# Gated experts, attention and routed experts on one core: x1's return moved ahead of expert 6's stores, output positions held in registers, and a new VectorE order in attention with v's bias folded

## The chip, the cores and the metric

One core of one Trainium2 chip runs one launch. The metric is the device time in microseconds (us). Engines: PE is TensorE, ACT is ScalarE, DVE is VectorE, POOL is GpSimd, SP is SyncE (it only issues DMAs). A "q" behind an engine's name is its instruction queue (register work, DMA issues).

## The reference

```python
x = x + attention(gated_ffn(x, type))                 # 64 sequences of 64 tokens, width 256, 16 heads, causal
x = x + moe(shared_and_typed_ffn(x, type))            # 3 shared and 2 typed passes, 4 gates
# attention:
q, k, v = x @ Wq.T + bq, x @ Wk.T + bk, x @ Wv.T + bv
o = softmax(q k / 4, causal) @ v
return o @ Wo.T + bo
# moe: a three-layer router, top 2 of 8 experts, at most 10 tokens of a sequence per expert
out = sum(scale * (relu(x @ eW1 + eb1) @ eW2 + eb2))  # over the two chosen experts
```

Since every row of the softmax sums to 1, v's bias adds the same vector `bv @ Wo.T` to every token of attention's output.

## The kernel before, in words

Each f32 operand is held as two f16 parts, a high part that ScalarE makes and a low part (value minus high) that VectorE makes; a product is three matmuls (high x high, high x low, low x high). The kernel goes through stages: the first gated pass over all tokens, the typed pass, attention, three shared passes and the typed one, the router, the dispatch, the eight experts, the combination.

**Attention** takes 16 chunks of four sequences (256 tokens) in a software pipeline, an order written out by hand for each engine, `for i in range(-1, NA + 2)`: in round i PE computes chunk i's scores (L748, L752), q and k of chunk i + 1 (`projection`, L735), the sums of chunk i - 1 (L799), the turned scores of chunk i (L767, L862, L778), the output product of chunk i - 2 (L735 again, after `normalisers_turned`, L808), the values of chunk i - 1 (L820) and v of chunk i (L829). L862, a small matmul, comes once a round.
- ScalarE: `o_high` (L1168), `v_high` (L1174), `qk_high` for q and k (L1152), the exponentials (L1160, L1161), x1's high part (L1204), `y_high` (L1147) for two chunks ahead.
- VectorE: `probs_low` of the last round (L1571), `row_max` (L1575), `1/sum` (L1603), two small ones (L1606, L1608), then o's low part (L1612), v's (L1618), q's and k's (`qk_low`, L1581), `k_parity` (L1588), x1 (L1630), `probs_low` (L1571), the normalised o (L1637) and x1's low part (L1641).
- POOL: `normalisers_wide` (L421), then y of two chunks ahead (`weighted`, L323, twice, and L412) and its low part (L416).
- SP: `q_blocks` (L530) writes q's parts as four DMAs into blocks that the next round's scores read; then the next y inputs (L523, L524), the store of x1 to DRAM (L540) and four loads of x (L466).
`o_high` and the low part of o add v's bias (`ab[:, 2, m]`) in two instructions each, one for each half of the width.

**Experts.** Expert e's hidden layer (L1001) goes through ScalarE (L1286, L1287) and VectorE (L1786) into the second product (L1013). Its 640 result rows are five tiles, three after the first half (8 of 16 steps) and two after the second. Each tile is scaled by VectorE (L1777), converted by ScalarE (L1308) and VectorE (L1780), and stored to SBUF by four DMAs, two of SP and two of POOL (L367, `expert_store`). There are four tile buffers, so tile 4 uses that of tile 0: `eout` makes L1308 of tile 4 wait until tile 0's stores have landed. POOL's queue also holds the fetches of the next weights into `wstage` (L394), which VectorE's L1799 releases (`w_ready`). Ahead of expert 7's stores POOL loads x1 back from DRAM, four DMAs of 1 MB (L445): two into `wstage`, two into the slots of expert 6's weights.

**Output.** In 4 x 8 groups PE multiplies the stored rows by the combination weights (L1037, 12 matmuls a group), VectorE adds x1 (L1817, two a group), and 64 stores of 64 KB follow, 24 from SP, 20 each from ACT and POOL. The sequences were sorted by type, so each store reads its place from a table: `out_store` does the load (L373), waits for the group (L374) and issues the DMA (L375), in a hardware loop over q. VectorE may write a buffer of `yo` again when the stores of the same group of q - 1 have landed.

## Time and profile before

| | |
|---|---|
| median of 3 runs | 2545.57 us (2543.66 to 2547.62) |
| the profiled execution | 2548.03 us |
| its span in the trace | 2546.5 us |
| PE busy | 2368.0 us, 93% |
| DVE, ACT, POOL busy | 1209.9, 1100.2, 169.7 us |

The span is what the profiler recorded of one execution; the 1.5 us between it and that execution's own time lie around it. Busy time doesn't count register work and DMA issues.

### The profile page before, as it was taken

What the parts mean: (1) busy time and instruction counts of PE and PEld (TensorE: products, weight loads), DVE (VectorE), ACT (ScalarE), POOL (GpSimd) and SP (SyncE); (2) the same over time, 40 slices, a digit from 0 to 9 for tenths busy, and PEclk for the clock granted to TensorE, in tenths of its full rate; (3) what the DMA queues carried; (4) which work ended last, traced back from release to release, by engine and by line L of the source; (5) the groups of instructions that cost most, each with busy time, mean ns of one, the idle gap of its engine ahead of it and who ended that gap; (6) DMA issues with size and microseconds to landing.
All of it is one profiled execution on the core that took longest, in us unless ns stands there. A gap on an engine that the chain in (4) does not pass through costs nothing.

```text
span 2546.5 us, 51783 instructions
## 1 busy us (share of the span) xinstructions
PE 2368.0 (93%) x18863; PEld 1561.2 (61%) x18880; DVE 1209.9 (48%) x2301; ACT 1100.2 (43%) x2097; POOL 169.7 (7%) x240
## 2 busy tenths in 40 slices
PE   6999999996888899999999999997999999589994
PEld 2444688885777444444447888884444444367774
DVE  5553455447988442332323333334343443685553
ACT  3553455444666342332323333332334433487761
POOL 0000000004332000000000000000000000002222
PEclk9999999998999899999999999997999999669996
DMA  3330111002332230120101000002111110017655
GB/s 117 100 99 33 46 50 50 17 23 69 93 86 69 89 115 33 50 74 25 58 25 42 29 13 12 13 12 71 50 50 33 33 33 0 1 50 93 92 79 120
DMA packets 139501, 136.80 MB, mean 54 GB/s; under 512 B 75872, under 2 KB 121952, under 8 KB 132960
## 3 DMA queue, kind: packets, MB, share of 16 engines
q1 hardware_dynamic: 125440, 76.93, 11.8%
q0 software_dynamic: 10896, 55.58, 8.0%
q8 instruction: 94, 1.54, 0.3%
q10 hardware_dynamic: 3024, 2.36, 0.3%
q14 instruction: 47, 0.39, 0.1%
HBM read 90.80 MB, written 34.60 MB: 49 GB/s over the span
## 4 chain that ended last, share of the span: by engine, by line
PE 82%; DVE 5%; ACT 4%; DMA 3%; issue 3%; SPq 2%; POOL 1%; POOLq 0%; DVEq 0%; ACTq 0%
PE ps L653 30%; PE ps L670 24%; PE ps L902 13%; PE ps L1013 3%; PE ps L1001 3%; PE ps L891 3%; DMA arena<-arena 1%; PE ps L735 1%; DMA arena<-misc 1%; ACT misc L1161 1%; PE ps L767 1%; ACT arena L1160 1%; SPq L466 1%; SPq L530 1%; PE ps L916 1%
## 5 line engine op out<-in xcount | busy, mean ns | idle before, releaser
L653 PE MATMUL ps<-xh,arena 128*128 (+1 forms) x5376 | 907.5, 312 | 18.3 <-DVE xh L1403 10.4
L670 PE MATMUL ps<-misc,arena 128*128 128x256 f16 (+1 forms) x4128 | 727.5, 313 | 10.4 <-DVE misc L1471 7.4
L653 PEld LDWEIGHTS ps<-xh,arena 128*128 (+1 forms) x5376 | 527.5, 98 | 289.4 <-issue 25.9
L670 PEld LDWEIGHTS ps<-misc,arena 128*128 (+1 forms) x4128 | 403.2, 98 | 224.3 <-issue 10.5
L1475 DVE SCALAR_TENSOR_TENSOR misc<-ps,misc 128x256 f16<-128x256 f32 (+1 forms) x480 | 254.9, 531 | 542.1 <-ACT misc L1093 541.2
L1093 ACT ACTIVATE misc<-ps 128x256 f16<-128x256 f32 (+1 forms) x480 | 225.0, 469 | 552.8 <-PE ps L653 552.8
L902 PE MATMUL ps<-arena 128*128 128x512 f16 x1536 | 332.8, 379 | 0.0
L902 PEld LDWEIGHTS ps<-arena 128*128 128x128 f16 x1536 | 149.8, 98 | 179.5
L1686 DVE TENSOR_TENSOR arena<-misc,arena 128x512 f16<-128x512 f32 x128 | 88.6, 692 | 253.7 <-ACT arena L1231 253.7
L1469 DVE TENSOR_TENSOR arena<-ps,misc 128x256 f32<-128x256 f32 (+1 forms) x208 | 105.2, 506 | 145.9 <-ACT misc L1089 144.9
L1230 ACT ACTIVATE misc<-ps,bias 128x512 f32<-128x512 f32 x128 | 87.8, 686 | 187.1 <-PE ps L902 181.2
L1089 ACT ACTIVATE misc<-ps 128x256 f32<-128x256 f32 (+1 forms) x208 | 93.5, 449 | 164.3 <-PE ps L653 164.2
L1471 DVE TENSOR_TENSOR misc<-arena,misc 128x256 f16<-128x256 f32 (+1 forms) x208 | 105.6, 508 | 114.0 <-ACT misc L1091 114.0
L1091 ACT ACTIVATE misc<-arena 128x256 f16<-128x256 f32 (+1 forms) x208 | 100.2, 482 | 127.6 <-DVE arena L1469 127.6
L1013 PE MATMUL ps<-arena,misc 128*128 128x256 f16 x960 | 125.8, 273 | 10.2 <-DVE misc L1786 10.1
L1001 PE MATMUL ps<-arena 128*128 128x384 f16 (+1 forms) x768 | 127.7, 304 | 2.2 <-ACT arena L1264 2.2
L1013 PEld LDWEIGHTS ps<-arena,misc 128*128 128x128 f16 x960 | 91.5, 98 | 34.7 <-DVE misc L1786 18.4
L1786 DVE TENSOR_TENSOR misc<-misc 128x256 f16<-128x256 f32 (+1 forms) x128 | 62.7, 490 | 79.3 <-ACT misc L1287 79.3
L891 PE MATMUL ps<-xh,arena 128*128 (+1 forms) x384 | 85.6, 383 | 15.2 <-DVE xh L1670 15.2
L1001 PEld LDWEIGHTS ps<-arena 128*128 128x128 f16 x768 | 75.9, 99 | 26.8 <-issue 2.8
L1459 DVE SCALAR_TENSOR_TENSOR arena<-wstage,arena 128x512 f16<-128x512 f32 x124 | 85.0, 686 | 12.5 <-ACT arena L1079 9.9
L735 PE MATMUL ps<-arena 128*128 128x256 f16 x576 | 76.6, 287 | 13.3 <-POOL arena L416 10.0
(235 smaller groups left out, 2033.1 us busy)
## 6 DMA issues: line engine op xcount, KB each, us to landing
wstage<-in_m_w POOLq DMA_DIRECT2D x16, 1024.0 KB, 5.2
arena<-src_d SPq DMA_DIRECT2D x64, 256.0 KB, 3.7
src_d<-misc SPq DMA_DIRECT2D x24, 512.0 KB, 3.1
wstage<-in_c_wi POOLq DMA_DIRECT2D x6, 1024.0 KB, 5.7
wstage<-in_r_w POOLq DMA_DIRECT2D x5, 1024.0 KB, 5.3
cexp_d<-misc SPq DMA_DIRECT2D x18, 256.0 KB, 2.5
src_d<-misc SPq DMA_DIRECT2D x18, 256.0 KB, 2.5
cshare_d<-misc SPq DMA_DIRECT2D x8, 512.0 KB, 3.1
```

The source lines that it names most:

```text
L653: last = mm(ps[:, bank, col:col + p.n], weight(off, half, g, wp, k * F + f * 128), xh[:, xp, k, ds(start, p.n)], start=(k == 0 and n == 0) ...
L670: last = mm(ps[:, 4 + 2 * half + m, 0:p.n], weight(place[0], half, 2 if p.gated else 1, wp, f * D + m * 128), hid[:, st % 4, hp, 0:p.n], s ...
L735: last = mm(dst, w16(ATTN_W, wp, (w * KC + k) * D + m * 128), data(xp, k), start=(k == 0 and j == 0), stop=(k == KC - 1 and j == 2))
L891: last = mm(ps[:, f % 4, :], w16(R_W1, wp, k * F + f * 128), xh[:, xp, k, ds(c * 512, 512)], start=(k == 0 and n == 0), stop=(k == KC - 1 ...
L902: last = mm(ps[:, 4 + fo % 2, :], w16(R_W2[k // 2], wp, (k % 2) * F + fo * 128), h1[:, k, xp, :], start=(k == 0 and n == 0), stop=(k == FC ...
L1001: last = mm(ps[:, (e * 16 + st) % 3, 0:n], w16(MOE_W[e % 2][0], wp, k * F + f * 128), xe[:, xp, k, e * PER_E + c0:e * PER_E + c0 + n], sta ...
L1013: last = mm(ps[:, 3 + t, 0:D], hid[:, st % 4, hp, i_t * 128:(i_t + 1) * 128], w16(MOE_W[e % 2][1], wp, f * D, D), start=(f == 0 and j == 0 ...
L1091: fn(hid[:, st % 4, 0, 0:p.n], p.fbuf(st), ACT.Copy).then_inc(p.hi, 1)
L1093: fn(hid[:, st % 4, 0, 0:p.n], ps[:, bank, col:col + p.n], ACT.Relu).then_inc(p.hi, 1)
L1469: v.tensor_tensor(p.fbuf(st), src, p.gbuf(st), ALU.mult).then_inc(p.mul, 1)
L1471: v.tensor_tensor(hid[:, st % 4, 1, 0:p.n], p.fbuf(st), hid[:, st % 4, 0, 0:p.n], ALU.subtract).then_inc(p.h, 1)
L1475: v.scalar_tensor_tensor(hid[:, st % 4, 1, 0:p.n], src, 0.0, hid[:, st % 4, 0, 0:p.n], ALU.max, ALU.subtract).then_inc(p.h, 1)
```

## The change

1. x1's first two loads go out on POOL ahead of expert 6's stores, once all weights are split; its last two between tile 2 and tile 3 of expert 6, once that expert's products are done.
2. `out_stores` replaces `out_store` and the hardware loops: each of the three queues first loads all its positions into registers, then goes through waits and DMAs with constant targets.
3. In attention VectorE's `qk_low` for q comes ahead of the low parts of o and v. v's bias is no longer added to o: 8 small matmuls multiply it by Wo before the loop, and VectorE adds the sum to bo. The high and the low part of o are one instruction each, without a bias.
4. `y_high(1)` moves from before attention's loop to the end of its first round.

```diff
--- before.py
+++ after.py
@@ -163,6 +163,8 @@
         rs = small[:, 64:96]
         rs_wide = region(SHIFT_SLOT, 2048, F32, 4096)
         ones_e = small[:, 122:123].bitcast(F16)
+        bv2 = small[:, 123:125].bitcast(F16).rearrange("p (k h) -> p k h", k=KC)
+        bv_sum = small[:, 125:127]
 
         h1 = region(H1_SLOT, 16384, F16).rearrange("p (f h n) -> p f h n", f=FC, h=2)
         h2 = region(H2_SLOT, 16384, F16).rearrange("p (f h n) -> p f h n", f=FC, h=2)
@@ -367,13 +369,16 @@
                 queue.dma_start(ebf[j][slot:slot + 1, :, :], eo[lo:lo + 32, t % 4, :, :].rearrange("p h n -> p (h n)")
                                 ).then_inc(s[f"{stored}{t % 4}"], 16)
 
-        def out_store(queue, stored, q, n):
-
-            u = n // 2
-            b = queue.value_load(tbl[0:1, ds(q * 16 + (n + T_PERM), 1)], min_val=0, max_val=B - 1)
-            queue.wait_ge(s["fin"], q * 8 + (u + 1))
-            queue.dma_start(a["out"][ds(b, 1)].rearrange("b p (k n) -> p (b k) n", k=KC),
-                            yo[:, u, n % 2, :, :]).then_inc(s[f"{stored}{u // 2}"], 16)
+        def out_stores(queue, stored, first):
+
+            places = [(q, n) for q in range(NP // 8) for n in range(first, 16, 3)]
+            batch = [queue.value_load(tbl[0:1, T_PERM + q * 16 + n:T_PERM + q * 16 + n + 1], min_val=0, max_val=B - 1)
+                     for q, n in places]
+            for (q, n), b in zip(places, batch):
+                u = n // 2
+                queue.wait_ge(s["fin"], q * 8 + (u + 1))
+                queue.dma_start(a["out"][ds(b, 1)].rearrange("b p (k n) -> p (b k) n", k=KC),
+                                yo[:, u, n % 2, :, :]).then_inc(s[f"{stored}{u // 2}"], 16)
 
         block = ctx.enter_context(nc.Block())
 
@@ -433,25 +438,27 @@
             for i in range(16, FIRST_MOE + 2):
                 fetch(i)
 
+            def x1_back(q):
+                pool.dma_start(x1f[q], x1_d[:, :, q * 1024:(q + 1) * 1024]).then_inc(s[f"x1_in{q}"], 16)
+
             for e in range(NE):
                 for i in range(FIRST_MOE + 2 * e + 2, min(FIRST_MOE + 2 * e + 4, len(loads))):
                     fetch(i)
-                if e == NE - 1:
-                    for q in range(4):
-                        if q == 0:
-                            pool.wait_ge(s["w_ready"], len(loads))
-                        if q == 2:
-                            pool.wait_ge(s["m_out"], 2 * (NE - 1))
-                        pool.dma_start(x1f[q], x1_d[:, :, q * 1024:(q + 1) * 1024]).then_inc(s[f"x1_in{q}"], 16)
+                if e == NE - 2:
+                    pool.wait_ge(s["w_ready"], len(loads))
+                    x1_back(0)
+                    x1_back(1)
                 for t in range(5):
+                    if e == NE - 2 and t == 3:
+                        pool.wait_ge(s["m_out"], 2 * (NE - 1))
+                        x1_back(2)
+                        x1_back(3)
                     pool.wait_ge(s["eo_lo"], e * 5 + (t + 1))
                     expert_store(pool, "eo_sp", e, t, 1)
 
 
 
-            with pool.Fori(0, NP // 8) as q:
-                for n in range(2, 16, 3):
-                    out_store(pool, "fin_sp", q, n)
+            out_stores(pool, "fin_sp", 2)
 
 
         @block.sync
@@ -582,9 +589,7 @@
                     sp.wait_ge(s["eo_lo"], e * 5 + (t + 1))
                     expert_store(sp, "eo_st", e, t, 0)
 
-            with sp.Fori(0, NP // 8) as q:
-                for n in range(0, 16, 3):
-                    out_store(sp, "fin_st", q, n)
+            out_stores(sp, "fin_st", 0)
             for g in range(4):
                 sp.wait_ge(s[f"fin_st{g}"], 16 * FIN_ST[g] * (NP // 8))
                 sp.wait_ge(s[f"fin_sp{g}"], 16 * FIN_SP[g] * (NP // 8))
@@ -838,6 +843,12 @@
                 last.then_inc(s["wo_mm"], 1)
 
             pe.wait_ge(s["w_ready"], 12)
+            for m in range(2):
+                for wp in range(2):
+                    col = (m * 2 + wp) * 2
+                    for k in range(KC):
+                        mm(ps[:, 6, col:col + 2], w16(ATTN_W, wp, (3 * KC + k) * D + m * 128), bv2[:, k, :],
+                           start=(k == 0), stop=(k == KC - 1))
             for i in range(-1, NA + 2):
                 here, ahead = 0 <= i < NA, i + 1 < NA
                 if here:
@@ -1164,9 +1175,7 @@
                 act.wait_ge(s["norm"], 2 * c + 2)
                 if c >= 1:
                     act.wait_ge(s["wo_mm"], c)
-                for m in range(KC):
-                    last = fn(oh_[:, 0, m, :], o_f[:, m, :], ACT.Identity, bias=ab[:, 2, m:m + 1])
-                last.then_inc(s["o_hi"], 1)
+                fn(oh_[:, 0, :, :], o_f, ACT.Copy).then_inc(s["o_hi"], 1)
 
             def v_high(c):
                 act.wait_ge(s["v_mm"], c + 1)
@@ -1174,8 +1183,7 @@
                     last = fn(vb(0, j), vp(j), ACT.Copy)
                 last.then_inc(s["v_hi"], 1)
 
-            for c in range(2):
-                y_high(c)
+            y_high(0)
             for i in range(-1, NA + 2):
                 if 0 <= i - 2 < NA:
                     o_high(i - 2)
@@ -1202,7 +1210,7 @@
                 if 0 <= i - 2 < NA:
                     act.wait_ge(s["x1"], i - 1)
                     fn(xh[:, 0, :, ds((i - 2) * CH, CH)], x1, ACT.Copy, scale=SX).then_inc(s["x1_hi"], 1)
-                if 2 <= i + 2 < NA:
+                if i + 2 < NA:
                     y_high(i + 2)
 
             for p in es:
@@ -1327,9 +1335,7 @@
             eout(NE - 1, 1)
 
 
-            with act.Fori(0, NP // 8) as q:
-                for n in range(1, 16, 3):
-                    out_store(act, "fin_st", q, n)
+            out_stores(act, "fin_st", 1)
 
 
         @block.vector
@@ -1450,7 +1456,9 @@
 
             def bias_scale():
                 dve.wait_ge(s["bias_in"], 32)
-                v.tensor_scalar(bias[:, 0:6], bias[:, 0:6], SQ, None, ALU.mult)
+                link(v.tensor_scalar(bias[:, 0:6], bias[:, 0:6], SQ, None, ALU.mult))
+                link(v.tensor_copy(bv2[:, :, 0], ab[:, 2, :]))
+                v.tensor_tensor(bv2[:, :, 1], ab[:, 2, :], bv2[:, :, 0], ALU.subtract)
                 v.tensor_scalar(bias[:, 8:88], bias[:, 8:88], SR, None, ALU.mult).then_inc(s["consts"], 1)
 
             def weight_low(i, q):
@@ -1592,6 +1600,10 @@
             v.memset(qbd_all, 0.0)
             v.memset(vbd_all, 0.0)
             selectors()
+
+            dve.wait_ge(s["qk_mm"], 1)
+            link(v.reduce_sum(bv_sum, ps[:, 6, 0:8].rearrange("p (m n) -> p m n", m=2), AX.X))
+            v.scalar_tensor_tensor(ab[:, 3, :], bv_sum, 1 / (SQ * SA), ab[:, 3, :], ALU.mult, ALU.add)
             for i in range(-1, NA + 2):
                 if 0 <= i - 1 < NA:
                     probs_low(i - 1, 1)
@@ -1606,19 +1618,17 @@
                     v.tensor_copy(mxb[:, 0:32], mx).then_inc(s["mx"], 1)
                     dve.wait_ge(s["mx"], 4 * i + 3)
                     v.tensor_tensor(mxb[:, 32:64], mx, mxb[:, 0:32], ALU.subtract).then_inc(s["mx"], 1)
+                if i + 1 < NA:
+                    qk_low(i + 1, 0, qh)
                 if 0 <= i - 2 < NA:
                     dve.wait_ge(s["o_hi"], i - 1)
-                    for m in range(KC):
-                        last = v.scalar_tensor_tensor(oh_[:, 1, m, :], o_f[:, m, :], ab[:, 2, m:m + 1],
-                                                      oh_[:, 0, m, :], ALU.add, ALU.subtract)
-                    last.then_inc(s["o_lo"], 1)
+                    v.tensor_tensor(oh_[:, 1, :, :], o_f, oh_[:, 0, :, :], ALU.subtract).then_inc(s["o_lo"], 1)
                 if 0 <= i - 1 < NA:
                     dve.wait_ge(s["v_hi"], i)
                     for j in range(2):
                         last = v.tensor_tensor(vb(1, j), vp(j), vb(0, j), ALU.subtract)
                     last.then_inc(s["v_lo"], 1)
                 if i + 1 < NA:
-                    qk_low(i + 1, 0, qh)
                     qk_low(i + 1, 1, kh)
                     k_parity(i + 1)
                 if 0 <= i - 2 < NA:
```

## Rows read from the trace of the kernel before

**Rows 1.** The page, busy time of each engine, share of the span, instructions.
```profile
PE 2368.0 (93%) x18863; PEld 1561.2 (61%) x18880; DVE 1209.9 (48%) x2301; ACT 1100.2 (43%) x2097; POOL 169.7 (7%) x240
```
**Rows 2.** The chain of waits over the end: start us, us, what.
```profile
2486.28 18.75 DMA arena<-misc
...
2505.13 0.42 ACT misc L1308
...
2506.79 2.21 issue
...
2512.50 1.45 PE ps L1037 x24
```
**Rows 3.** The timeline of experts 6 and 7: start us, us, engine, line.
```profile
2453.67 1.22 DVE L1799 SCALAR_TENSOR_TENSOR arena<-wstage,arena 128x1024 f16<-128x1024 f32 x1
...
2469.21 0.42 DVE L1777 SCALAR_TENSOR_TENSOR misc<-ps,misc 128x256 f32<-128x256 f32 x1
...
2474.12 1.47 POOL L445 DMA_DIRECT2D wstage<-x_d  x2
...
2496.50 0.42 DVE L1777 SCALAR_TENSOR_TENSOR misc<-ps,misc 128x256 f32<-128x256 f32 x1
```
**Rows 4.** DMA issues from 2440 us on: KB each, median us to landing.
```profile
wstage<-x_d POOLq DMA_DIRECT2D x2, 1024.0 KB, 9.7
...
out_x<-misc SPq DMA_DIRECT2D x24, 64.0 KB, 1.8
```
**Rows 5.** The timeline of SP in the output stage.
```profile
2514.06 30.46 SPq L375 DMA_DIRECT2D out_x<-misc  x24
```
**Rows 6.** The output stage by stretch: us, PE, PEld, DVE, ACT, POOL busy, PEclk, DMA share, GB/s.
```profile
2512.50:2533.20 20.70, 20.64 (x384) 20.48 (x384) 10.88 (x48) 0.00 (x0) 7.38 (x14) 0.50 0.46 132
```
**Rows 7.** The same view over ten rounds of attention.
```profile
641.50:792.73 151.23, 134.97 (x2761) 117.22 (x2770) 139.00 (x201) 99.11 (x180) 55.52 (x52) 0.98 0.37 89
```
**Rows 8.** Waits from 590 to 850 us: us in total, times, longest.
```profile
PE ps L752 <- DMA arena<-arena: 23.3, 11, 7.3
```
**Rows 9.** The timeline of L862 on PE.
```profile
700.83 0.24 PE L862 MATMUL ps<-identb,small 128*64 128x128 bf16 x1
...
718.16 0.24 PE L862 MATMUL ps<-identb,small 128*64 128x128 bf16 x1
...
731.72 0.24 PE L862 MATMUL ps<-identb,small 128*64 128x128 bf16 x1
```
**Rows 10.** The timeline of one round with a wait; in brackets idle time and releaser.
```profile
697.52 0.84 ACT L1152 ACTIVATE arena<-ps,bias 128x256 f16<-128x256 f32 x2 [1.16 <-PE ps L735]
...
699.53 2.03 DVE L1612 SCALAR_TENSOR_TENSOR arena<-arena,bias 128x256 f16<-128x256 f32 x2
...
700.02 0.54 SPq L466 DMA_DIRECT2D arena<-in_x  x1
700.05 2.43 POOL L323 TENSOR_TENSOR arena<-arena,gates 128x512 f32<-128x512 f32 x2
...
702.90 1.66 DVE L1581 SCALAR_TENSOR_TENSOR arena<-ps,bias,arena 128x256 f16<-128x256 f32 x4
...
703.81 2.69 SPq L530 DMA_DIRECT2D arena<-arena  x4
...
710.14 0.39 PE L752 MATMUL ps<-arena 128*128 128x128 f16 x4 [2.47 <-DMA arena<-arena]
```
**Rows 11.** Instructions of line L373: duration ns min/median/max, first and last start.
```profile
L373 SPq FUSED_REGOPS  x44: 51/152/167, 2507.7 to 2543.7; - x44
...
L373 SPq TENSOR_LOAD <-tbl x24: 264/269/583, 2507.4 to 2543.4; - x24
```
**Rows 12.** L1612's instructions: duration ns min/median/max, first and last start.
```profile
L1612 DVE SCALAR_TENSOR_TENSOR arena<-arena,bias x32: 385/833/1277, 625.9 to 839.8; 128x256 f16<-128x256 f32 x32
```
**Rows 13.** The timeline: a POOL pair beside no L1612.
```profile
595.94 2.07 POOL L323 TENSOR_TENSOR arena<-arena,gates 128x512 f32<-128x512 f32 x2 [7.53 <-DMA arena<-cshare_d]
```
**Rows 14.** The page's costliest groups: busy us, mean ns, idle before.
```profile
L1686 DVE TENSOR_TENSOR arena<-misc,arena 128x512 f16<-128x512 f32 x128 | 88.6, 692 | 253.7 <-ACT arena L1231 253.7
```

## The prediction

> **What bounds the kernel now.** I read the page first, for which engine is full: PE, at 93% of the span [rows 1]. So the change can pay only where PE waits, and the views by stretch and by wait show two such places in the code that it touches.
>
> The first is the end. The chain of waits holds one transfer item of 18.75 us, then ScalarE's conversion L1308 at 2505.13, 2.21 us in which POOL's sequencer waits for nothing shown, and PE's first output matmuls at 2512.50 [rows 2]. The timeline shows why: POOL issues x1's four 1 MB loads from 2474.12, ahead of expert 7's stores, and 2 MB of them take 9.7 us to land [rows 3, 4]. Expert 7's last tile is ready on VectorE at 2496.50 [rows 3], but its buffer is shared with tile 0, whose store lies behind x1. After that the stores to the output set the end: SP issues its 24 in 30.46 us, one per 1.31 us, while PE is done with its 384 short matmuls after 20.64 us, at a granted clock of 0.50, the lower of its two levels (1.2 GHz) [rows 5, 6].
>
> The second is attention. From the mask transposition L862 of 641.50 to the one ten later, 151.23 us pass: 15.12 us each, with VectorE busy 13.90 and PE 13.50 [rows 7]. PE waits 23.3 us in 11 places for the DMAs that spread q into blocks [rows 8]. Where it waits 2.47 us, the period is 17.33 us (700.83 to 718.16); where it doesn't, 13.56 [rows 9, 10].
>
> **Part 1: x1 ahead of expert 6's stores.** The staging buffers are free when VectorE has split expert 7's weights, 2453.67 + 1.22 = 2454.9; the second pair when expert 6 is through, 2469.2 [rows 3]. POOL is idle at both. Each pair takes some 10 us [rows 4], so they land near 2465 and 2480. An expert takes 2496.5 - 2469.2 = 27 us and has no tile before its middle, so expert 7's first store, near 2485, finds the DMA engines free. Expert 6's stores now share them with x1; the cover is that its tile 0, stored just after 2455, has 14.3 us (2454.9 to 2469.2) until tile 4 wants the buffer, and a pair is through in 9.7. Were it not, ScalarE would stand there and PE behind it. So L1308 of the last tile follows VectorE's 2496.50 + 0.42 at once, at 2497.0 instead of 2505.13: 8.1 us. PE's start keeps its distance of 7.4 us from L1308 and moves to 2504.3, with POOL's 2.2 us gap still in it; without the gap it is 2502.1.
>
> **Part 2: positions in registers.** On SP a position costs 0.27 us of load and 0.15 of register work; with the second register step (0.05, the minimum of its row) and the check and gaps between instructions, which I estimate at 0.14, that is 0.61 of the 1.31 us [rows 11]. The constant target of the wait saves a register step too, 0.07 with its gap. A store is then 0.63 us. But the loads stand in front of the first store now: 24 x 0.53 (no address step) = 12.7 us on SP. The first load comes 2507.4 - 2505.1 = 2.3 us after L1308 [rows 2, 11], so they run from 2499.2 to 2511.9. PE's first results are there at 2505.5, so SP is 6.4 us late; ACT and POOL have 20 each. From 2511.9, 24 x 0.63 = 15.1 us gives 2527.0. PE is no earlier: eight groups' buffers are free again when SP's first stores have landed (2515), and the last 16 of the 32 groups take 16 x 0.65 = 10.4 us at the lower clock, to 2525.9 with VectorE, then the last store. From the last issue to the end are 2.0 us now (2544.5 to 2546.5) [rows 5], so 2529.0. The output goes out at twice the rate, and the DMA engines, at 0.46 share in the stretch of before [rows 6], come near full: I add 1.3 us (an estimate: two thirds of a landing of 1.8 us [rows 4]), 2530.3. **The end gains 16.2 us.** Bounds: loads in 0.3 us each and no gap at POOL, 20.5; stores held at 190 GB/s by the transfers (132 now [rows 6]), 10.
> The row prices a load at 0.27 us. The Trainium skill, page "DMA: Bandwidth & Descriptors", section "Latency and other measured facts", puts the floor of such a load at about 600 ns, which speaks against 24 of them in a row: by it SP would be ready near 2520 and the end would gain about 8 us. The trace disagrees in the median (0.269 us; only the longest of the 24, 0.583, is near [rows 11]), so the sum goes by the row; rival (b) holds the other case.
>
> **Part 3: attention.** VectorE's part for q moves ahead of o's and v's low parts. ScalarE has q ready at 698.36, VectorE is free at 699.53, so it need not wait [rows 10]. The part for q starts 3.4 us earlier (702.90 to 699.5), and SP, which finishes the x loads at 700.56, can issue the blocks at 700.6 instead of 703.81 [rows 10]. Issue to scores is 6.3 us [rows 10], so they are ready at 706.9, where PE without a wait comes at 710.14 - 2.47 = 707.7. The 23.3 us of DMA waits go [rows 8]. What is late next is VectorE: 13.90 us busy per round.
>
> There v's bias counts. Two L1612 of 128x256 take 2.03 us, although one takes 0.385 alone [rows 10, 12]: POOL's L323 runs beside them, and is itself slowed from 2.07 to 2.43 for a pair [rows 10, 13]. One 128x512 subtraction with two SBUF inputs takes 0.69 alone [rows 14]. The unknown is its price beside POOL. If two engines take turns (POOL's extra 0.36 is one L1612), one instruction pays at most one turn (1.28 - 0.385 = 0.9), half of it on average: 1.1 us. If they share a rate, it is 0.69 x 2.03/0.77 = 1.8. Below: 0.69. Above: 0.69 + 2.43 = 3.1, shut out for all of POOL's pair. I take 1.1, as the 0.36 is so near to one instruction; VectorE saves 0.9 and needs 13.0 plus small gaps.
> By the Trainium skill, page "SBUF — State Buffer", section "Who interferes with whom", whichever of two such instructions starts first holds the shared ports until it ends; that is the reading by turns, with which the sum is 13.2 us, where the one by rate gives the 6 of rival (a).
>
> v_low now ends about when it did (0.9 for q, minus 0.9), so the output product isn't delayed. ScalarE's one operation for two hides in its idle time. The floor is then the unstalled 13.56; for jitter, and for SP, whose x loads end just when the blocks are due, I take 13.8: 151.2 - 138 = 13.2 us. The last two rounds, where nothing hides o's parts, may give some tenths more, which I set against small losses. **Attention gains 13.2 us.** Bounds: 3 (VectorE still sets the pace, part of the waits stay) and 16.
> At nothing: the 8 matmuls for the folded bias (PE waits for POOL's first y then; without that cover 8 x 0.054 = 0.4 us, the price of the smallest matmuls [rows 6]), the two extra operations in the first pass and two before the loop (tiny beside L1612's 0.385 alone [rows 12]; without cover 1 us in all; they lie in a pass that PE bounds, and beside ScalarE's first q), and the later y_high(1), wanted only a round later.
>
> **The sum.** Against the profiled execution (2548.03 us, span 2546.5): 2548.0 - 16.2 - 13.2 = 2518.6. The median of the runs is 2.5 lower, 2545.57: forecast **2516.2**.
>
> **The rivals.**
> (a) Attention stays bound by VectorE: the merged subtraction pays by rate, 1.8 for 2.03, so 13.7 busy and with the gaps 14.5 us per round, and only 6 us come. For it: the 13.90 already busy. Against: 0.36 us on POOL. Total 2523.
> (b) The loads in front of the stores, or the DMA engines, take back half of the end: 8 to 10 us there, total 2523.
> (c) The moved stores don't do what they say: expert 7's tile 0 still waits, because SP's queue is held by x1's pair, and attention only shifts its wait: 10 us in all, 2536.
> (d) Slower: the low part of o, now behind q's, is shut out for 3.1 us. PE's output product then waits over 2 us in each round, and every round takes the 17.33 us of the worst one now: 14 x 2.2 = 31 us lost, 16 gained at the end, 2560. It decides once the product waits as long as the 2.47 us of [rows 10]; against it, VectorE began its L1612 1.3 us ahead of PE's L862 (699.53, 700.83), and the extra would be 1.1.
>
> **Chances.** Forecast 0.66, (a) 0.16, (b) 0.10, (c) 0.05, (d) 0.03. The range takes in the first three with their bounds, 2508 to 2529. A measurement of this kernel tells 0.2% (5 us) from no change: faster 0.95, same 0.02, slower 0.03.
>
> **What would show it.** Right: x1's first pair issued before expert 6's tile 0, its second near that expert's end; L1308 of the last tile within 1 us of VectorE; PE's output matmuls 7 to 8 us after it; 24 table loads in a row on SP, then stores 0.6 to 0.7 us apart; L862 every 13.6 to 13.9 us; waits of the scores on DMA under 5 us in all; the merged subtraction at 0.7 to 1.5 us. Wrong: stores still 1 us apart or landing after 4 us; PE waiting for the low part of o; a period above 14.3.

## The result and the profile after

| | before | after |
|---|---|---|
| median of 5 runs | 2545.57 us (2543.66 to 2547.62) | 2534.38 us (2532.39 to 2540.72) |
| ratio, 95% interval | | 0.9965 [0.995, 0.998] |
| the profiled execution, its span | 2548.03, 2546.5 us | 2540.72, 2539.1 us |

The change gains 11.2 us by the medians, 7.4 by the two spans; 29.4 were forecast, and 2534.4 lies above the range of 2508 to 2529. On another chip (`after_again` below) it came to 0.9973 [0.9962, 0.9983]. Its line numbers differ: L862 is now L873, L1001 L1012, L1308 L1316, L1037 L1048, L1817 L1827, L735 L740, L375 L380. The page answers to [rows 1]:

```profile
PE 2370.9 (93%) x18887; PEld 1558.8 (61%) x18888; DVE 1201.2 (47%) x2289; ACT 1095.5 (43%) x2080; POOL 171.2 (7%) x239
```

**Attention.** Ten rounds after L873 of 644.44, where 151.23 us stood in [rows 7]:

```profile
644.44:786.04 141.60, 134.82 (x2771) 115.43 (x2770) 130.82 (x191) 96.14 (x170) 55.70 (x51) 1.00 0.38 95
```

14.16 us a round. VectorE's 13.08 is what was forecast (13.0), and PE's waits for the q blocks are gone. Of the 6.8 us in which PE is idle in these ten rounds, 3.6 are waits for POOL's low part of y, and beside 3.0 the view of the waits (us in total, times, longest) names no releaser. POOL stands behind ScalarE, and ScalarE stands at L1201 until SP's loads of x have landed: 11.6 us in nine places, where the ten rounds of before have 4.7 us in four. The median load of x takes 2.2 us to land in both kernels; in the shorter round ScalarE comes for it earlier.

```profile
POOL arena L421 <- ACT arena L1158: 48.0, 10, 5.4
...
ACT arena L1201 <- DMA arena<-in_x: 11.6, 9, 2.0
...
PE ps L740 <- POOL arena L421: 3.6, 5, 1.2
```

**The experts.** POOL's and SP's timelines around experts 6 and 7, then ScalarE's. Both x1 pairs go out where the forecast has them. But tile 0's stores, issued from 2453.27 to 2454.58, have landed only 17 us later: ScalarE waits 4.25 us before expert 6's tile 4, and 4.52 before expert 7's tile 0, which wants that tile 4's buffer.

```profile
2451.59 1.48 POOL L442 DMA_DIRECT2D wstage<-x_d  x2 [8.87 <-DVE arena L1809]
2453.54 0.53 POOL L369 DMA_DIRECT2D xh<-misc  x1 [0.48 <-DVE misc L1790]
2454.06 0.52 POOL L369 DMA_DIRECT2D arena<-misc  x1
...
2464.98 1.48 POOL L442 DMA_DIRECT2D arena<-x_d  x2 [6.51 <-PE ps L1024]
```
```profile
2471.68 0.42 ACT L1316 ACTIVATE misc<-misc 128x256 f16<-128x256 f32 x1 [4.25 <-DMA arena<-misc]
2484.81 0.42 ACT L1316 ACTIVATE misc<-misc 128x256 f16<-128x256 f32 x1 [4.52 <-DMA arena<-misc]
...
2497.22 0.42 ACT L1316 ACTIVATE misc<-misc 128x256 f16<-128x256 f32 x1 [0.83 <-DVE misc L1787]
```

**The end.** In the chain of waits the last tile's L1316 is no longer late (2495.98 and 2497.22 instead of 2505.13 [rows 2]), yet PE starts at 2510.40, 13.2 us behind it instead of 7.4:

```profile
2498.39 0.50 POOL xh L369
2498.88 2.21 issue
2501.12 9.09 DMA arena<-misc
2510.20 0.20 issue
2510.40 16.17 PE ps L1048 x300
...
2526.96 4.38 DMA out_x<-misc
```

SP's row answers to [rows 5]: 24 stores in 21.40 us instead of 30.46, 2.2 us behind PE's start. Its 24 loads start between 2499.3 and 2511.9 (second fence, one line's instructions), wholly inside the wait for that landing but for about a microsecond. The output stage (third fence, as [rows 6]) moves 175 GB/s instead of 132.

```profile
2512.63 21.40 SPq L380 DMA_DIRECT2D out_x<-misc  x24
```
```profile
L375 SPq TENSOR_LOAD <-tbl x24: 261/267/292, 2499.3 to 2511.9; - x24
```
```profile
2510.40:2531.00 20.60, 20.60 (x384) 20.47 (x384) 12.76 (x56) 0.00 (x0) 9.22 (x17) 0.50 0.62 175
```

From SP's last issue (2534.0) to the end of the span are 5.1 us, where the kernel before has 2.0. The end is POOL's. The last long instruction of its queue, a DRAIN, starts right behind POOL's last output store and takes 5.13 us, while SP's queue is through 2.7 us before the end (ns, then the first and last start; the third line is of the kernel before):

```profile
L76 POOLq DRAIN  x1: 5130/5130/5130, 2533.8 to 2533.8; - x1
L76 SPq DRAIN  x1: 7/7/7, 2536.4 to 2536.4; - x1
L76 POOLq DRAIN  x1: 4995/4995/4995, 2541.2 to 2541.2; - x1
```

In all 18 traces it takes 4.8 to 5.1 us. The last output store has landed 3.0 us before the end. In the kernel before POOL had its last store out 2.8 us ahead of SP. With the loops the span ended 1.7 to 2.6 us after the last issue of any queue (six traces); with the positions in registers the queues finish together, and it ended 4.5 to 4.8 us after (twelve traces). What POOL does in that time isn't shown.

**By stretch.** Single executions of one kernel differ by 0.3% (2532.4 to 2540.7 us after the change), as much as a part is worth. So the experiments are read by stretches of the trace, cut at the first or last start of a line's instructions (the page's lines of the kernel after; a run's own numbers differ by a few). A: first L721 to first L873, the start of attention. B: to the last L740, attention. C: to the last L728, the shared passes. D: first to last L1012, the experts. E: to the last L1316. F: to PE's first L1048. G: to the end of the span. The 564 to 569 us ahead of A and the 528 to 530 between C and D are left out. Microseconds, good to 0.1; the ratio is to the kernel before on the same chip.

| kernel | A | B | C | D | E | F | G | ratio [95%] |
|---|---|---|---|---|---|---|---|---|
| before | 33.3 | 241.1 | 897.8 | 224.1 | 12.4 | 7.4 | 34.0 | 1 |
| after | 36.4 | 232.3 | 900.0 | 228.1 | 4.2 | 13.2 | 28.7 | 0.9965 [0.995, 0.998] |
| after_again | 34.4 | 232.9 | 899.2 | 232.4 | 4.2 | 12.9 | 28.4 | 0.9973 [0.9962, 0.9983] |
| p1_x1 | 31.9 | 249.3 | 896.1 | 226.3 | 4.2 | 13.2 | 33.9 | 1.0002 [0.9988, 1.0015] |
| p2_loads | 30.6 | 241.3 | 898.2 | 223.0 | 12.9 | 7.3 | 31.3 | 0.9993 [0.998, 1.0005] |
| p3_attn | 33.3 | 235.8 | 898.4 | 223.5 | 13.9 | 7.4 | 34.4 | 0.9989 [0.9977, 1.0001] |
| order_only | 33.2 | 235.9 | 895.8 | 224.2 | 12.5 | 7.4 | 34.0 | 0.9972 [0.9962, 0.9982] |
| bias_only | 34.7 | 233.8 | 899.9 | 223.5 | 13.9 | 7.3 | 34.3 | 1.0000 [0.9989, 1.0011] |
| x1_34 | 34.6 | 232.1 | 900.1 | 229.2 | 4.2 | 13.2 | 28.3 | 0.9969 [0.9955, 0.9983] |
| no_x1 | 34.4 | 234.7 | 899.9 | 224.8 | 4.2 | 13.2 | 28.2 | 0.9952 [0.9937, 0.9968] |
| x1_late | 34.4 | 233.9 | 899.9 | 222.0 | 4.3 | 13.5 | 28.1 | 0.9954 [0.994, 0.9968] |
| hoist | 34.6 | 232.8 | 898.6 | 232.0 | 4.2 | 13.1 | 28.4 | 0.9967 [0.9954, 0.998] |
| late_bias | 33.0 | 233.4 | 898.8 | 228.8 | 4.2 | 13.2 | 27.2 | 0.9983 [0.9973, 0.9993] |
| best | 34.3 | 232.8 | 898.7 | 223.4 | 4.2 | 13.6 | 28.4 | 0.9955 [0.994, 0.997] |
| skip3 | 34.6 | 232.9 | 899.0 | 227.2 | 4.3 | 7.9 | 30.2 | one run |
| p2_hoist | 30.7 | 245.3 | 897.7 | 223.0 | 12.5 | 7.4 | 29.5 | one run |
| order_mm | 34.3 | 237.6 | 899.2 | 222.5 | 13.4 | 7.4 | 34.3 | one run |
| order_late | 30.4 | 234.8 | 899.1 | 224.4 | 4.2 | 15.3 | 28.4 | 0.9945 [0.993, 0.9959] |

Where the code is the same, A, B and C repeat within 3 to 4 us (B of the old order within 8), D with x1 early within 6 and otherwise within 2.5, E, F and G within 1.5 (F of 15.3 aside). One trace of a kernel thus settles a step of F or G, but not one of 1 to 3 us in A, B or C.

### The profile page after: what moved, and what is told of

Read it like the earlier page. It is cut to its first block, busy times and chain, and to the rows that moved or that the text cites. A ratio compares the mean times of both kernels' runs of the same rounds, so it can differ in the third digit from the quotient of the medians.

```text
span 2539.1 us, 51629 instructions
## 1 busy us (share of the span) xinstructions
PE 2370.9 (93%) x18887; PEld 1558.8 (61%) x18888; DVE 1201.2 (47%) x2289; ACT 1095.5 (43%) x2080; POOL 171.2 (7%) x239
## 4 chain that ended last, share of the span: by engine, by line
PE 82%; DVE 5%; ACT 4%; DMA 3%; issue 3%; SPq 2%; POOL 0%; DVEq 0%; ACTq 0%; POOLq 0%
PE ps L658 31%; PE ps L675 24%; PE ps L913 13%; PE ps L902 3%; PE ps L1024 3%; PE ps L1012 3%; DMA arena<-misc 1%; DVE arena L1762 1%; DMA arena<-in_x 1%; ACT misc L1172 1%; SPq L473 1%; PE ps L740 1%; SPq L472 1%; ACT arena L1171 1%; PE ps L772 1%
## 5 line engine op out<-in xcount | busy, mean ns | idle before, releaser
L675 PEld LDWEIGHTS ps<-misc,arena 128*128 (+1 forms) x4128 | 402.8, 98 | 227.1 <-issue 13.6
L1024 PE MATMUL ps<-arena,misc 128*128 128x256 f16 x960 | 125.9, 273 | 13.9 <-DVE misc L1796 13.8
L1012 PE MATMUL ps<-arena 128*128 128x384 f16 (+1 forms) x768 | 127.7, 304 | 2.2 <-ACT arena L1272 2.2
L740 PE MATMUL ps<-arena 128*128 128x256 f16 x576 | 75.6, 285 | 18.1 <-POOL arena L421 14.7
L1012 PEld LDWEIGHTS ps<-arena 128*128 128x128 f16 x768 | 75.9, 99 | 26.8 <-issue 2.8
L1467 DVE SCALAR_TENSOR_TENSOR arena<-wstage,arena 128x512 f16<-128x512 f32 x124 | 85.0, 685 | 12.5 <-ACT arena L1090 9.9
```

Of the source, the lines that this page charges most:

```text
L675: last = mm(ps[:, 4 + 2 * half + m, 0:p.n], weight(place[0], half, 2 if p.gated else 1, wp, f * D + m * 128), hid[:, st % 4, hp, 0:p.n], s ...
L740: last = mm(dst, w16(ATTN_W, wp, (w * KC + k) * D + m * 128), data(xp, k), start=(k == 0 and j == 0), stop=(k == KC - 1 and j == 2))
L1012: last = mm(ps[:, (e * 16 + st) % 3, 0:n], w16(MOE_W[e % 2][0], wp, k * F + f * 128), xe[:, xp, k, e * PER_E + c0:e * PER_E + c0 + n], sta ...
L1024: last = mm(ps[:, 3 + t, 0:D], hid[:, st % 4, hp, i_t * 128:(i_t + 1) * 128], w16(MOE_W[e % 2][1], wp, f * D, D), start=(f == 0 and j == 0 ...
```

## The experiments

**The parts alone** (`p1_x1`, `p2_loads`, `p3_attn`: the kernel before with the diff's first, second, third and fourth point respectively, the last two together). Then x1's pairs moved between the stores (`x1_34`), the changed kernel with

```diff
-                if e == NE - 2:
-                    pool.wait_ge(s["w_ready"], len(loads))
-                    x1_back(0)
-                    x1_back(1)
                 for t in range(5):
                     if e == NE - 2 and t == 3:
+                        pool.wait_ge(s["w_ready"], len(loads))
+                        x1_back(0)
+                        x1_back(1)
+                    if e == NE - 2 and t == 4:
                         pool.wait_ge(s["m_out"], 2 * (NE - 1))
```

> The kernel before with the moved loads of x1 alone. Theory A (the DMA engines, not the order of the waits, set when the last expert tile's stores land; the moved loads stand in front of expert 6's stores): expert 6's tile 4 waits some 4 us at ScalarE for tile 0's store, TensorE starts the output 1 to 2 us later than in the kernel before, total 2545.6 + 1.6 = about 2547. Theory B (the step as forecast; in the changed kernel it only met an unlucky transfer): the last L1308 8 us earlier, output start 8 us earlier, about 2537.5.

> The kernel before with the moved output-position loads and unrolled stores alone. Theory A: the loads in front of the first store lie inside the wait for the last landing (17 us) but for about 1 us, the stores then go at TensorE's pace plus 4 us of waits for output buffers: the 34.0 us from TensorE's start to the end become 28.7, total about 2540.3. Theory B (SyncE's 12.7 us of loads stand in front of everything as forecast): the gain is at most 8.1 us less what the loads hold up; with the last expert store issued at 2507.2 the first output store would come at 2520 instead of 2514, stores at 0.63 us each, about 2539 to 2541 too, so what tells them apart is the time of the first output store: 2514 to 2515 (A) or 2520 (B).

> The kernel before with both attention parts alone (VectorE's order, and v's bias folded into the output projection's bias). Theory A (9.6 us gained over ten rounds, 3 lost at the start, 2 to 3 lost again in the first shared pass to the clock): 3.7 us, total about 2541.9. Theory B (the start's and the first pass's losses in the one trace were chance): 8 to 10 us, total 2536 to 2538. Forecast: 13.2 us, 2532.4.

> The changed kernel with x1's first pair issued behind the stores of expert 6's tile 2 instead of ahead of tile 0's, the second pair between the stores of tiles 3 and 4. Theory A (tile 0's stores were held up by x1 ahead of them in the DMA engines): ScalarE's 4.2 us wait before expert 6's tile 4 goes, the last tile comes out 4 us earlier, total 4 us below the changed kernel's 2534.4, about 2530. Rival (the stores' own landing of 9 to 11 us sets it, whoever stands ahead): the same wait moves to another tile, no change, 2534.

`p1_x1` shows theory A's mechanism: E falls by 8.2 us, F rises by 5.8, D by 2.2, ratio 1.0002. (The 1 to 2 us by which PE was to start later are -0.2 in D, E and F together.) ScalarE's waits in it and in `x1_34`:

```profile
2479.91 0.42 ACT L1312 ACTIVATE misc<-misc 128x256 f16<-128x256 f32 x1 [3.08 <-DMA arena<-misc]
2493.59 0.42 ACT L1312 ACTIVATE misc<-misc 128x256 f16<-128x256 f32 x1 [5.08 <-DMA arena<-misc]
```
```profile
2485.45 0.42 ACT L1316 ACTIVATE misc<-misc 128x256 f16<-128x256 f32 x1 [8.90 <-DMA arena<-misc]
```

In `x1_34` tile 4 no longer waits, but expert 7's tile 0 waits 8.9 us, for the stores that now stand behind x1's second pair. Theory A had the cause and not the result; the gain of 4 us did not come, the rival was right that the wait moves.

`p2_loads`: the medians differ by 2.8 us, where A and B both had 5 to 6, and B's clue was there: SP's first store 7.3 us behind VectorE's first product, and VectorE idle for 4.78 us until it.

```profile
2516.59 17.79 SPq L378 DMA_DIRECT2D out_x<-misc  x24
```
```profile
2509.33 1.06 DVE L1814 SCALAR_TENSOR_TENSOR misc<-ps,wstage 128x128 f32<-128x128 f32 x4 [7.40 <-PE ps L1036]
...
2519.00 1.68 DVE L1814 SCALAR_TENSOR_TENSOR misc<-ps,wstage 128x128 f32<-128x128 f32 x8 [4.78 <-PE ps L1036]
```

Where the landing is early (F of 7.3) the loads have no cover and take back half of the gain: G 31.3 against 28.7. `p3_attn`: B 235.8, ratio 0.9989, nearer to theory A's 3.7 us than to B's 8; its interval, like that of `p2_loads`, takes in no change.

**x1 away, x1 late, loads early, bias sums late.** Four edits of the changed kernel: `no_x1` issues none of the four loads and waits for none, so its output lacks x1; `x1_late`:

```diff
                     expert_store(pool, "eo_sp", e, t, 1)
+                if e == NE - 2:
+                    pool.wait_ge(s["w_ready"], len(loads))
+                    x1_back(0)
+                    x1_back(1)
+            x1_back(2)
+            x1_back(3)
```

`hoist` does the loads of SP and POOL ahead of `for e in range(NE)`; `late_bias` moves VectorE's two operations behind the first `k_parity`:

```diff
-            dve.wait_ge(s["qk_mm"], 1)
-            link(v.reduce_sum(bv_sum, ...))
-            v.scalar_tensor_tensor(ab[:, 3, :], bv_sum, ...)
...
                     k_parity(i + 1)
+                if i == -1:
+                    link(v.reduce_sum(bv_sum, ...))
+                    v.scalar_tensor_tensor(ab[:, 3, :], bv_sum, ...)
```

> The changed kernel without any of the four loads that bring x1 back (the last additions then use whatever the buffers hold, so the output lacks x1). Theory A (x1's 2 MB and the expert stores share DMA engines that are near their limit, so wherever x1 goes it moves a wait): the waits of ScalarE's L1316 for a landing, 4.2 us in the changed kernel and 8.9 with x1 moved between the stores, are below 1 us, the stretch from expert 6's first matmul group to the last (228.1 us over all experts, 223.5 before) comes to 223 to 224, and the span is 5 us below the changed kernel's. If TensorE still starts the output some 13 us behind the last conversion, the stores' landing at the end owes nothing to x1; if 7 to 9, x1 delayed it. Rival (the stores alone are slow): the 4 us wait stays.

> The changed kernel with x1's first pair behind expert 6's last stores (where both pairs were before the change) and its second pair behind expert 7's last stores. Theory A: expert 6's tile 4 no longer waits (4 us), the 1 MB at 2469 is landed before expert 7's stores, and the second pair lies in the idle DMA time while TensorE waits for the last stores; it is wanted only by the output's second half, 10 us after TensorE's start. Experts 4 us shorter, last conversion at 2493, TensorE starts at 2506, span 2535, total some 4 us below the changed kernel. Rival: the second pair on POOL's queue slows the last landing or VectorE waits for it in the middle of the output (at most 10 us for a pair): no gain or 3 us worse.

> The changed kernel with the output positions of SyncE and GpSimd loaded ahead of the eight experts; ScalarE's stay. Theory A (the loads are covered by the wait for the last landing but for 1 us): first SyncE output store within 0.4 us of VectorE's first two products instead of 1.3 us behind the start of the first (2511.30 to 2512.63), waits for free output buffers 4 us -> 2 to 3, TensorE's start unchanged, from its start to the end 27 to 28 us instead of 28.7. Theory B, the forecast's (the loads stand in front, 12 us): 8 us and more gained.

> The changed kernel with VectorE's two operations for the folded bias moved from ahead of the attention loop to behind its first pass's low parts. Theory A (the two, 1.2 us with the one slowed beside GpSimd, delay q's low part and with it the first blocks and scores): from the first gate-side matmul to the first softmax turn (36.4, 34.6, 33.3 us in three runs with the fold, 33.3, 31.9, 30.6 without) 0.7 to 1.2 us off the mean of 34.8. Rival (the new matmuls or the later y_high make the 3 us): still about 34.8.

`no_x1`: D 224.8, no wait of L1316 (this run's L1308) for a landing from 2430 us on, span 5.1 us lower. So x1 costs D its 4 us. The other traces agree: the six with x1 ahead of expert 6's stores have both waits, 7.2 to 9.5 us together, and a mean D of 229.1; the seven with x1 where it was have 223.4. But F stays 13.2, so the late landing at the end is not x1's. Nor is it POOL's late last issue. In this run that store went out at 2494.43, 0.65 us behind the one before it, and PE still started at 2505.77:

```profile
2493.78 0.50 POOL L369 DMA_DIRECT2D xh<-misc  x1 [0.26 <-DVE misc L1782]
2494.43 0.50 POOL L369 DMA_DIRECT2D arena<-misc  x1
```
```profile
2505.77 10.40 PE L1040 MATMUL ps<-arena,xh 80*128 80x64 f16 x192 [14.89 <-DMA arena<-misc]
```

`x1_late` does as well as leaving x1 out: D 222.0 without a wait, F 13.5, and VectorE never waits for the second pair. It gains 12.2 us, against the changed kernel's 11.2 and 7.1; these come from different chips, and the intervals of the ratios overlap, so the step is shown by D and not by the medians.

`hoist`: first SP store 0.66 us behind the first product (2511.71, 2511.05), G 28.4. That is 0.3 us: theory B is out, and A had hoped for 0.7 to 1.7. `late_bias`: A 33.0, 1.8 us under the mean of 34.8 where theory A had 0.7 to 1.2; but `best` has the same edit and A 34.3. It is not settled by the one run, and `order_mm` below speaks for the rival.

**Order alone, fold alone, a repeat, and a version that joins the good parts** (`best`: `x1_late`, `hoist` and `late_bias` together). `order_only` has only the move of `qk_low(i + 1, 0, qh)` and of `y_high(1)`; `bias_only` the rest of the attention part.

> The changed kernel once more, beside the others on one chip. Its first trace gave 36.4 us from the first gate-side matmul to the first softmax turn and 228.1 us of experts; four variants of it with the same code in the first stretch gave 33.3 to 34.6. If the first 36.4 was chance, 34 to 35 here; the experts again 227 to 229; total 0.9965 of the kernel before, within 0.0015.

> The kernel before with VectorE's order changed alone (q's low part ahead of o's, the second y behind the first pass). Theory A (the order takes the 23 us of waits for the q blocks away, the fold only shortens ScalarE's and VectorE's work): attention's loop 241 to 243 us in runs of the old order, 232.1 to 235.8 with both, comes to 234 to 237; the first stretch stays at 31 to 33. Rival (the shorter o work is what ends the waits): 240 or more.

> The kernel before with v's bias folded alone, VectorE's order as it was. Theory A: the loop gains about 1 us per round only where o's low part stood ahead of q's, so q's blocks come 0.5 to 1 us earlier: loop 236 to 240; the first stretch 1.2 to 3 us longer (33 to 35). Rival (the fold carries the gain): loop 235 or less.

> The changed kernel with three edits: x1's first pair behind expert 6's stores and its second behind expert 7's (4 to 6 us in the experts, measured), output positions of SyncE and GpSimd loaded ahead of the experts (0.3 to 1 us), the two operations of the folded bias behind the first pass (1 to 2 us). Expected: 6 to 8 us under the changed kernel, about 0.9935 of the kernel before. If the sum fails, the experts' stretch (222 us) and the first one (33) say which part did.

`after_again`: A is 34.4 as expected, so 2 us of the 36.4 were chance; D is 232.4, above the 227 to 229 expected; the ratio is within its band.

The two attention edits are substitutes. The scores' waits on DMA in the loop, 16.1 us in ten places in the kernel before (23.3 with the first), are absent with the new order and 4.5 with the fold:

```profile
PE ps L752 <- DMA arena<-arena: 16.1, 10, 2.5
```
```profile
PE ps L750 <- DMA arena<-arena: 4.5, 4, 1.6
```

B is 235.9 and 233.8 with one and 232 to 236 with both: once the blocks are in time, a second way of getting them in time is worth little. So `order_only` came out by its theory A, and `bias_only` in the loop by its rival (235 or less). The order alone measures 0.9972, as much as the whole change; the fold alone 1.0000. In its trace A, C and E give back 5.0 of B's 7.3 us, each by no more than such stretches vary. The merged low part of o takes 1.33 us beside POOL and 0.63 alone (duration ns min/median/max), 1.1 in `bias_only`:

```profile
L1625 DVE TENSOR_TENSOR arena<-arena x16: 628/1334/1335, 629.7 to 833.4; 128x512 f16<-128x512 f32 x16
```
```profile
L1623 DVE TENSOR_TENSOR arena<-arena x16: 629/1099/1101, 627.4 to 833.6; 128x512 f16<-128x512 f32 x16
```

The traces show why the two differ. In the changed kernel it starts at 629.67, inside a POOL instruction of 629.40 to 630.46, and ends at 631.01; POOL's next one, beside which it then runs, takes 1.51 us instead of 1.06. In `bias_only` it starts at 627.45, inside the copy of 627.34 to 628.00, and ends at 628.55. Each time it ends 0.55 us after the instruction that POOL had begun before it.

`best`: 0.9955 [0.994, 0.997] where 0.9935 was expected. D and G came as measured before, A did not.

**The landing, the loads uncovered, and the fold's matmuls.** `skip3`: the changed kernel without the stores of expert 7's tile 3 (`if e == NE - 1 and t == 3: continue` on SP and POOL, PE's waits for that buffer lowered by 32). `p2_hoist`: `p2_loads` with `hoist`. `order_mm`: `order_only` with the fold's eight matmuls and the splitting of v's bias, and nothing else of it. `order_late`: `order_only` with `out_stores`, `x1_late` and `hoist`.

> The changed kernel without the four stores of expert 7's tile 3 (its rows of the experts' output stay unwritten, so the output lacks them). Theory A (the last eight 32 KB stores, each into one partition, drain one after the other at some 1.6 us each, whenever the last one was issued: 13.2 us after the last conversion with eight of them behind each other in five kernels, 7.4 with four): TensorE starts the output 6.5 to 8 us behind the last conversion, span 5 to 6 us below the changed kernel's. Rival (the landing is late because GpSimd's last store is issued 2.2 us late and then takes 9 us by itself): still 11 us or more.

> The kernel before with moved output-position loads (as in the change) and SyncE's and GpSimd's hoisted on ahead of the experts. In the kernel before the last landing comes 7.4 us behind the last conversion, too short a cover for the 12.7 us of loads: with the loads at the end, SyncE's first output store came 7.3 us behind VectorE's first product and VectorE waited 4.8 us in the first half. Theory A: hoisted, SyncE's first output store comes 0.7 us behind the first product, that wait goes, and from TensorE's start to the end 31.3 becomes 28 to 28.5. Rival (the wait is for the stores' landings, not the loads): still 31.

> The kernel before with VectorE's new order, and with the fold's eight small matmuls alone (their product is not used; v's bias stays where it was). In nine runs with the fold the first q blocks landed 6.0 to 6.7 us after their issue (first scores), in four without it 4.3 to 4.7; moving VectorE's two operations did not change it. Theory A (TensorE's matmuls ahead of the loop do it, by moving its program or what is fetched beside the blocks): 6 us or more here, first stretch 34 to 35. Rival (it comes from the rest of the fold): 4.3 to 4.7, first stretch 31 to 33.

> VectorE's new order and the output positions in registers, without the fold of v's bias, with x1's pairs behind the last stores of experts 6 and 7, and SyncE's and GpSimd's position loads ahead of the experts. The new order alone measured 0.9972 of the kernel before; its trace has 224.2 us of experts (222 to 223.4 with x1 late), 19.9 from the last matmul group to the output's start (17.8) and 34.0 from there to the end (28.4): 2538.2 - 1.5 - 2.1 - 5.6 = 2529 by the span, 0.9935 of the kernel before, 1 to 2 us under the version with the fold. If the fold's shorter work is needed after all, the same as that version (0.9955).

`skip3`: F 7.9 with four stores ahead of the landing, 13.2 with eight. SP issued its first of the four at 2495.96, 7.1 us before PE starts.

```profile
2495.96 0.50 SPq L369 DMA_DIRECT2D xh<-misc  x1
...
2503.05 10.40 PE L1052 MATMUL ps<-arena,xh 80*128 80x64 f16 x192 [9.73 <-DMA arena<-misc]
```

With eight, in `no_x1`, it is 13.5 us, to PE's 2505.77 above:

```profile
2492.28 0.50 SPq L369 DMA_DIRECT2D xh<-misc  x1
```

By these two traces each further 32 KB store adds 1.6 us, and theory A holds for the number of stores; whether they drain one after the other is not seen (see the last section). G is 30.2 here, between the 31.3 of `p2_loads` and the 28.4 of `after_again`: the shorter the landing, the less it covers the loads.

`p2_hoist`: the first store 0.67 us behind the first product, G 29.5 instead of 31.3. Uncovered, the 12.7 us of loads cost 1.8 us, less than expected (2.8 to 3.3), for stores' landings still hold VectorE (5.6 us in three places). `order_mm`: A 34.3 with the matmuls alone. The chain of waits there, and in `order_only`: the fourth q block lands after 3.94 us instead of 2.11.

```profile
587.82 3.94 DMA arena<-arena
591.76 0.05 issue
591.80 0.61 PE ps L749
```
```profile
589.00 2.11 DMA arena<-arena
591.11 0.05 issue
591.16 0.61 PE ps L748
```

So the eight matmuls alone bring the later landing; that they lengthen A rests on more traces than this one, for 1.1 us is within what A varies. In all twelve kernels with these matmuls the fourth block lands 3.8 to 4.2 us after its issue, in the four without them whose landings are on record after 2.1; from the first block's issue to the scores it is 6.0 to 7.1 us in the twelve and 4.3 to 5.1 in the six others. The matmuls run some 15 us before it and write nothing that it needs. What the view of the DMA queues (packets, MB, share) shows from 585.5 to 592 us of `order_mm`, and not beside `order_only`'s blocks, is one instruction transfer of 0.02 MB:

```profile
q1 hardware_dynamic: 2615, 0.75, 48.4%
q8 instruction: 1, 0.02, 0.9%
```

The same single transfer lies between the first block's issue and the scores in each of the twelve, and in none of the six. So it goes with the late block; that it holds the block up is still not shown, since no run moved it alone.

`order_late` measures 0.9945 [0.993, 0.9959], 14 us under the kernel before and the lowest ratio of all, although F was 15.3 (13.5 and 13.6 in `x1_late` and `best`, which also have x1's second pair behind the last stores; the difference isn't explained); 0.9935 was expected. Its interval is clear of `after_again`'s [0.9962, 0.9983], but not of the changed kernel's first [0.995, 0.998] nor of `best`'s.

## Why the prediction was wrong

Each of the three parts failed at a step of its own. By the two traced executions they lose 9.7 (part 1), 2.7 (part 2) and 9.5 us (part 3) against the forecast, 22 in all; the medians came 3.8 us better than these executions, which leaves the miss of 18.

**Part 1, the cover.** Expert 6's tile 0 "has 14.3 us (2454.9 to 2469.2) until tile 4 wants the buffer, and a pair is through in 9.7." The pair's own landing was used for a store that is issued behind it. The store needed 17 us. The step named its failure itself: "Were it not, ScalarE would stand there and PE behind it." It cost 4.0 us of D (228.1 instead of 224.1; 5.7 by the means above), and `no_x1` gives 3.3 of it back, `x1_late` all.

**Part 1, the distance.** "PE's start keeps its distance of 7.4 us from L1308." The 7.4 was the time of four stores, because tile 3's had long landed while tile 4 waited for x1. With the wait gone eight stand behind each other, and the distance is 13.2, with x1 or without (`no_x1`), and 7.9 where only four are left (`skip3`). So 5.8 of the 8.1 us are lost again, which none of the rivals had. The 8.1 itself was right (12.4 - 4.2 = 8.2), and part 1 is worth nothing: 1.0002.

**Part 2.** The 12.7 us of loads are right (12.6 from the first to the last). That they stand in front of the stores was wrong in the changed kernel, by the step above: the late landing covers them, and `hoist` finds 0.3 us. But the output gained 5.3 us (34.0 to 28.7), not 8.0 (34.0 to 2530.3 - 2504.3 = 26.0). From PE's start to SP's last issue are 23.6 us instead of 22.7: the stores start earlier but take 0.89 us each, not 0.63, for PE needs its 20.6 us at the lower clock and VectorE waits 3.8 us in two places for landed buffers. The other 1.8 us lie behind the last issue. The sum took the 2.0 us of [rows 5] and 1.3 for the transfers; 5.1 were measured, since POOL's DRAIN of 5.13 us now starts with the last stores. This is the step of the 7.4 us once more: a distance read behind SP's last store held only as long as POOL had finished earlier. That fewer or earlier stores on POOL would give it back is not tried. Part 2 alone, with nothing over its loads, gives 2.7.

**Part 3.** The term that failed is the round: 13.8 us, "the unstalled 13.56" and a little, were taken, 14.16 measured, 3.6 us over ten rounds. VectorE is not what sets it (13.08 us busy), and the waits of the scores are gone; single rounds of 13.56 us do occur (702.00 to 715.56). By the waits PE stands for POOL's low part of y behind ScalarE, whose wait for x had 4.7 us before and was not looked at, and in 3.0 us of idle time without a named cause. No run takes either away, so what sets 14.16 stays open. `order_only` and `bias_only` show besides that each edit alone ends most of the scores' waits, and that one alone leaves the loop at 234 to 236 (238 in `order_mm`) where both leave 232 to 236. Another 5.3 us are lost in A and C (36.4 and 900.0 instead of 33.3 and 897.8), which the sum had at nothing; under 1 us is left for the loop's other rounds.

The merged instruction was mis-sized as well, 1.33 for 1.1, and took 0.71 more than alone, one turn of POOL's at most. The Trainium skill, page "SBUF — State Buffer", section "Who interferes with whom", has it so: the instruction that starts second waits for the shared ports. The starts and ends above agree, so by turns was right, and the price depends on which instruction of POOL's is running; yet it didn't set the period. "At nothing" stood against the eight matmuls, and with them A is 34.3 instead of 33.2 (`order_mm`, `order_only`); over all runs A is 33.0 to 36.4 with them, 30.4 to 33.3 without. In C the kernels with the fold have 898.4 to 900.1, the others 895.8 to 899.2; whether that is more than chance stays open.

**The rivals.** Rival (c), 2536 with a chance of 0.05, was nearest in time and place: expert 7's tile 0 does wait for stores behind x1's pair, 4.52 us. Its reason, SP's queue, was wrong: SP issues the stores of tile 4 (2472.58) right after VectorE's low part, and it is their landing that takes long. Rival (b) had "or the DMA engines" and half of the end right (E, F and G gain 7.7 us of 16.2) and the loads wrong. Rival (d) needed PE to wait for the low part of o; it doesn't. The range took in one failure at a time; here every part fell short.

The median of 2534.4 thus is: 2545.6 + 1.6 (part 1) - 5.3 (part 2) - 3.7 (part 3, in the spans) = 2538.2 by the two traced executions; the medians are 3.8 better, within what single executions differ by.

## What to carry to other kernels

A distance read from a trace ("PE starts 7.4 us behind the conversion") belongs to the queue it was read in: before it is moved, count what stands in that queue, and what will once the wait ahead of it is gone. Two edits that end the same wait are not to be added; try each alone, since one may be the whole gain (here the order, 0.9972 of 0.9973) and the other none (the fold, 1.0000). Slow little stores and a 2 MB load on the same engines are best parted: the load goes where the queue is idle, here behind the last store. And when one queue gets faster, look at what the other queues still have to do after their last store: it may be what ends the kernel next.

## What the runs showed that was not expected

The last eight expert stores of 32 KB, each into a single partition, need 13.5 us, four need 7.1; the recorded packets of `no_x1` end near 2500, with the DMA share 0.03 from there on, and the landing is seen at 2505.8.

```profile
2496.00:2500.00 4.00, 0.00 (x0) 0.00 (x0) 0.00 (x0) 0.00 (x0) 0.00 (x0) 0.50 0.97 23
2500.00:2504.00 4.00, 0.00 (x0) 0.00 (x0) 0.00 (x0) 0.00 (x0) 0.00 (x0) 0.50 0.03 1
```

At a share of 0.97 they move 23 GB/s, the output stores 175 at 0.62. In `skip3` it is the same with four stores: the share is 0.00 from 2499 on, and the landing is seen at 2503.05. What holds the landing back after the last packet stays open, and since no run stores the same 32 KB into several partitions, so does whether the single partition makes them slow.

VectorE's tiny sum of 128x2 took 1.04 us in one execution, when it began 0.13 us behind an instruction of POOL (587.33), and 0.16 in the next, when it didn't. In the first it ended with POOL's instruction, at 588.50.

```profile
L1606 DVE SCALAR_TENSOR_TENSOR bias<-small,bias x1: 1042/1042/1042, 587.5 to 587.5; 128x2 f32<-128x2 f32 x1
```
```profile
L1606 DVE SCALAR_TENSOR_TENSOR bias<-small,bias x1: 161/161/161, 586.5 to 586.5; 128x2 f32<-128x2 f32 x1
```

A table load into a register takes 0.267 us on SP, here in the median of 24 in a row, under the floor of about 600 ns that the Trainium skill, page "DMA: Bandwidth & Descriptors", section "Latency and other measured facts", gives.
